# A decoder layer with a mixture of experts: one more expert pass between the last attention segments

## The reference

```
x = LN(x + self_attention(x))            # 16 heads of 16, causal window of 64
x = LN(x + cross_attention(x, ctx))      # relu on q, k, v; causal; + q; LN * gamma + beta
x = LN(x + experts(x))

# experts: tokens in 2 groups of 1024, 8 experts, top 2, capacity 160 per expert and group
pos      = place of each choice in its expert's queue, counted over the whole group
h        = relu(expert_in @ wi[e])       # 160 x 256 @ 256 x 1024
y        = h @ wo[e]                     # 160 x 1024 @ 1024 x 256
```

## Time and profile before

| | |
|---|---|
| median of three executions | 691.75 us (690.23 to 692.27) |
| the profiled execution's own time | 692.64 us |
| its span, first to last instruction | 690.6 us |
| mean granted TensorE clock | 0.909 of full speed |
| PE busy | 543.8 us, 79% |
| PEld busy | 421.6 us, 61% |
| DVE busy | 339.0 us, 49% |
| ACT busy | 218.3 us, 32% |
| POOL busy | 147.5 us, 21% |

### The profile page before, as it was taken

One profiled execution on the slowest core, in us unless ns is written; L12 is line 12 of the kernel. 1 busy time (PEld: TensorE's weight loads), 2 busy tenths in 40 slices (PEclk: granted clock), 3 DMA queues, 4 the chain that ended last, 5 costly groups with the idle time before them and its releaser, 6 DMA issues.

```text
span 690.6 us, 12843 instructions
## 1 busy us (share of the span) xinstructions
PE 543.8 (79%) x5092; PEld 421.6 (61%) x5092; DVE 339.0 (49%) x952; ACT 218.3 (32%) x491; POOL 147.5 (21%) x160
## 2 busy tenths in 40 slices
PE   5074939889898997997988668998687988998970
PEld 4052726656675765665666445777576866787860
DVE  3363615657577676776787547733333101232113
ACT  2000414354254453445445233453110100213103
POOL 4010003011021021031141650001111662322320
PEclk9577879999999999999999887999978989999995
DMA  4999654753935934935384462445555212688214
GB/s 109 202 181 131 211 85 65 96 59 63 121 45 84 113 44 74 113 47 79 48 108 72 84 160 60 152 170 178 203 180 181 62 36 58 191 251 282 32 13 131
DMA packets 56760, 78.97 MB, mean 114 GB/s; under 512 B 9294, under 2 KB 49357, under 8 KB 53628
## 3 DMA queue, kind: packets, MB, share of 16 engines
q1 hardware_dynamic: 42524, 39.64, 35.4%
q10 hardware_dynamic: 8032, 33.21, 15.3%
q0 software_dynamic: 6144, 5.29, 4.7%
HBM read 40.32 MB, written 13.74 MB: 78 GB/s over the span
## 4 chain that ended last, share of the span: by engine, by line
PE 33%; issue 8%; DVE 8%; DMA 3%; ACT 2%; SPq 1%; POOL 1%; ACTq 0%; another core or an unknown queue 0%; POOLq 0%; DVEq 0%
PE work L634 10%; PE work L648 8%; PE work L651 2%; PE work L442 2%; PE pv L560 2%; PE byk L496 1%; DVE negm L913 1%; PE work L436 1%; PE byk L492 1%; PE work L619 1%; DMA arena<-in_ffn_wi 1%; PE nat L496 1%; DVE r_c L984 1%; DVE stats_c L928 1%; PE work L599 1%
## 5 line engine op out<-in xcount | busy, mean ns | idle before, releaser
L913 DVE TENSOR_REDUCE negm<-nat 128x4 f32<-128x512 f32 (+2 forms) x192 | 120.5, 641 | 121.8 <-PE nat L496 116.6
L730 ACT ACTIVATE probs<-byk 128x512 f32<-128x512 f32 (+1 forms) x192 | 106.4, 563 | 131.1 <-PE byk L496 129.1
L496 PE MATMUL nat<-arena 96*128 96x128 bf16 (+2 forms) x512 | 74.9, 250 | 0.0
L496 PE MATMUL byk<-arena 99*128 99x128 bf16 (+2 forms) x512 | 73.1, 245 | 0.0
L1167 POOL TENSOR_TENSOR resk<-fk,parts_k 128x512 f32<-128x512 f32 x8 | 9.3, 1160 | 240.9 <-ACT fk L672 201.2
L492 PE MATMUL nat<-window_q,identb 128*128 128x384 bf16 (+1 forms) x96 | 36.5, 380 | 29.2 <-DMA arena<-parts_k 22.8
L496 PEld LDWEIGHTS nat<-arena 96*128 96x128 bf16 x512 | 47.6, 103 | 17.3 <-issue 3.9
L496 PEld LDWEIGHTS byk<-arena 99*128 99x128 bf16 x512 | 46.3, 100 | 18.6 <-issue 2.3
L492 PE MATMUL byk<-window_k,identb 128*128 128x384 bf16 (+1 forms) x96 | 34.5, 359 | 19.9 <-DMA arena<-mT 19.4
L634 PE MATMUL work<-woT,arena 128*128 128x160 f32 x256 | 46.5, 341 | 4.2 <-issue 4.0
L634 PE MATMUL work<-yn_T,arena 128*128 128x160 f32 x256 | 40.6, 313 | 10.6 <-DMA arena<-in_ffn_wi 6.0
(11 more groups left out here) (189 smaller groups left out, 951.5 us busy)
## 6 DMA issues: line engine op xcount, KB each, us to landing
arena<-parts_q SPq DMA_DIRECT2D x96, 128.0 KB, 5.0
arena<-parts_k SPq DMA_DIRECT2D x96, 128.0 KB, 5.3
arena<-in_ffn_wi ACTq DMA_DIRECT2D x12, 1024.0 KB, 4.9
arena<-in_ffn_wo ACTq DMA_DIRECT2D x12, 1024.0 KB, 8.2
expert_x<-fq ACTq DMA_DIRECT2D x1, 2600.0 KB, 12.6
v_s<-expert_x SPq DMA_DIRECT2D x20, 130.0 KB
xres<-in_x ACTq DMA_DIRECT2D x1, 2048.0 KB, 28.2
token_y<-xres SPq DMA_DIRECT2D x8, 256.0 KB, 2.2
```

The source lines that it names most:

```text
L496: last = nc.tensor.matmul(bank[:, i * w:(i + 1) * w], lhsT, rhs, start=False, stop=(i == heads - 1), skip_group_check=True)
L730: nc.scalar.activation(dst, src, ACT.Exp, scale=0.25).then_inc(exp_ready, 1)
L913: V.tensor_reduce(dst, src, AX, ALU.max, negate=True).then_inc(nat_free[job % 2], 1)
```

## The change

Passes now start at slots 187, 195, 204, 211 and then every 5.4. Pass 0 begins 8 slots earlier, pass 2 is complete in the table when unit 15's last scores are made (at 211), and pass 3 starts right there. Before, pass 2 was the one that stood across that point. The rows of passes 0 and 1 are fetched from slot 179 and 180 instead of 184.5 and 185.5.

Expert 3's weights go to slot 0, once pass 0 has ended, and no longer to slot 3. Expert 4 takes slot 3, once unit 15 has made its last scores; experts 5, 6 and 7 follow on passes 1, 2 and 3 in slots 1, 2 and 0. For the second group expert 7 is still in slot 0, 6 in 2, 5 in 1 and 4 in 3, and experts 3, 2, 1, 0 are loaded after passes 8 to 11. The list `WEIGHTS` holds (expert, slot, pass or none, pair) for each load in this order.

```diff
--- before.py
+++ after.py
@@ -55,6 +55,10 @@
 X_TURN = (1, 1, 1, 1, 2, 2, 2, 3)
 X_BEFORE = {4: 0, 5: 1, 6: 2, 7: 4}
 LOADS = ((-20, 0), (-17.3, 1), (-16, 2), (-5, 3), (-4, 4), (2, 5), (6, 6), (14, 7), (22, 8), (26, 9))
+
+
+WEIGHTS = [(0, 0, None, 0), (1, 1, None, 1), (2, 2, None, 2), (3, 0, 0, 0), (4, 3, None, 3), (5, 1, 1, 1), (6, 2, 2, 2), (7, 0, 3, 0),
+           (3, 0, 8, 0), (2, 2, 9, 2), (1, 1, 10, 1), (0, 3, 11, 3)]
 
 
 PASSES = [(e, 0) for e in range(E)] + [(e, 1) for e in reversed(range(E))]
@@ -106,7 +110,7 @@
             add(end + at, name, n)
         for i in range(TOPK * GT):
             add(end + 3.1 + 0.75 * i, "GS", n, i)
-    begin = [195, 203, 210]
+    begin = [187, 195, 204, 211]
     while len(begin) < len(PASSES) + 1:
         begin.append(begin[-1] + 5.4)
     for x, t in enumerate(begin):
@@ -114,15 +118,13 @@
             add(t, "H0", x)
             add(t + 2, "H1", x)
             add(t + 3.2, "H2", x)
-            add(184.5 + x if x < 2 else begin[x - 2] + 1.9, "EL", x)
+            add(179 + x if x < 2 else begin[x - 2] + 1.9, "EL", x)
             add(begin[0] - 1 if x == 0 else begin[x - 1] + 4, "XT", x)
         if x > 0:
             add(t + 0.8, "EY", x - 1)
             add(t + 1.5, "ES", x - 1)
-    for i in range(WSLOTS):
-        add(first_slot(12 + i) + 30.5, "WL", i)
-        add(begin[i + 1] + 1, "WL", i + WSLOTS)
-        add(begin[E + i + 1] + 1, "WL", E + i)
+    for i, (_, _, prior, pair) in enumerate(WEIGHTS):
+        add(first_slot(12 + pair) + 30.5 if prior is None else begin[prior + 1] + 1, "WL", i)
     for c in range(GB):
         add(begin[E] + 4.2 + 0.1 * c, "FL", 0, c)
         for at, name in ((2.6, "FM"), (2.8, "FR"), (4.5, "FF"), (4.6, "FN"), (4.9, "FS")):
@@ -136,20 +138,16 @@
 PLAN = in_order()
 
 
+def weights_of(x):
+
+    e, n = PASSES[x]
+    i = max(i for i, load in enumerate(WEIGHTS) if load[0] == e and (n == 1 or i < E))
+    return WEIGHTS[i][1], sum(load[1] == WEIGHTS[i][1] for load in WEIGHTS[:i + 1])
+
+
 WORK_SEGS = ("QS", "KS", "VS", "KC", "XC", "QC", "VC", "FQ", "XR", "RT", "MT", "YA", "YB", "Y2", "WO", "GP", "XT", "H0", "H1", "H2", "EY")
 WB = 3
 WORK_TURN = {seg[0:2]: (i % WB, i // WB) for i, seg in enumerate(seg for seg in PLAN if seg[0] in WORK_SEGS)}
-
-
-def weights_of(i):
-
-    e = i if i < E else 2 * WSLOTS + 3 - i
-    return e, e % WSLOTS
-
-
-def weight_turn(e, n):
-
-    return 1 if e < WSLOTS and n == 0 else 2 if e >= WSLOTS else 3
 
 
 def attention_and_experts(nc: bass.Bass, a, out):
@@ -623,33 +621,33 @@
...
                     if name == "H0":
-                        pe.wait_ge(wi_in[e % WSLOTS], 16 * weight_turn(e, n))
+                        pe.wait_ge(wi_in[place], 16 * turn)
                         emptied(pe, "XT", x)
...
@@ -786,13 +784,13 @@
                     nc.scalar.dma_start(wr[:, :, :], a["w_router"]).then_inc(wr_in, 16)
 
             def WL(i, n, layer, b):
-                if i < WSLOTS:
-                    last_t(act, 12 + i)
+                e, place, prior, pair = WEIGHTS[i]
+                if prior is None:
+                    last_t(act, 12 + pair)
                 else:
-                    computed(act, "EY", i - WSLOTS if i < E else i)
-                e, slot_of = weights_of(i)
-                nc.scalar.dma_start(wi[slot_of], a["ffn_wi"][e]).then_inc(wi_in[slot_of], 16)
-                nc.scalar.dma_start(wo[slot_of], a["ffn_wo"][e]).then_inc(wo_in[slot_of], 16)
+                    computed(act, "EY", prior)
+                nc.scalar.dma_start(wi[place], a["ffn_wi"][e]).then_inc(wi_in[place], 16)
+                nc.scalar.dma_start(wo[place], a["ffn_wo"][e]).then_inc(wo_in[place], 16)
 
             def clear(k, n, layer, b):
                 if b == 0:
```

More of the change, by code:

```diff
@@ L625, in handle @@
                 def handle(x, _, layer, b):
-                    e, n = PASSES[x]
+                    place, turn = weights_of(x)
                     if name == "H0":
-                        pe.wait_ge(wi_in[e % WSLOTS], 16 * weight_turn(e, n))
+                        pe.wait_ge(wi_in[place], 16 * turn)
                         emptied(pe, "XT", x)
@@ L640, in EY @@
             def EY(x, _, layer, b):
-                e, n = PASSES[x]
-                pe.wait_ge(wo_in[e % WSLOTS], 16 * weight_turn(e, n))
+                place, turn = weights_of(x)
+                pe.wait_ge(wo_in[place], 16 * turn)
                 for name in ("H0", "H1", "H2"):
@@ L647, in emit @@
                     for f in range(FC):
-                        nc.tensor.matmul(bank[:, 0:D], hT[x % 2][:, f, 0:P], wo[e % WSLOTS][:, f, :], start=(f == 0), stop=(f == FC - 1))
+                        nc.tensor.matmul(bank[:, 0:D], hT[x % 2][:, f, 0:P], wo[place][:, f, :], start=(f == 0), stop=(f == FC - 1))
                     for f in range(FC):
@@ L651, in emit @@
                             mm = nc.tensor.matmul(bank[32 * j:32 * j + REST, D:D + ZW], hT[x % 2][:, f, P:CAP],
-                                                  wo[e % WSLOTS][:, f, j * ZW:(j + 1) * ZW], start=(f == 0), stop=(f == FC - 1),
+                                                  wo[place][:, f, j * ZW:(j + 1) * ZW], start=(f == 0), stop=(f == FC - 1),
                                                   skip_group_check=True)
```

2 lines of the change are left out of this document (1 added, 1 removed).

## The result

The changed kernel took 695.86 us (median of nine runs, 691.85 to 700.2); the kernel before took 690.14 us beside it (median of nine, 686.19 to 699.24). The ratio is 1.009, with a 95% interval of 1.0059 to 1.0121: slower, by about 6 us. The time lies in the range that was given, but the forecast itself, no change at 692.4 us, was wrong. The profiled execution of the changed kernel took 697.16 us, its span is 694.2 us and its mean granted clock 0.895 (before: 692.64, 690.6 and 0.909).

What follows compares the result with a forecast made beforehand. The chain of rows from unit 15 sets pass 8's start, then PE alone bounds the tail. Links of +0.9, +0.6 and -1.8 us plus +1.0 for clock give +0.7: 691.75 to 692.4 us, range 688.8 to 696.5.

Steps and rivals of the forecast that it cites:

- first rival: Before unit 15's last scores: expert 3's load delays the maxima rows; +4.3 us, 696 us; 28% including any other longer link.
- a wait of `byk` for the maxima rows: Sign that the forecast is wrong: before unit 15's last scores, PE waits for that unit's maxima rows.
- last scores near 489.1 us: Sign that the forecast is right: unit 15's last scores come within 1.5 us of 489.1; after 492 means wrong.
- the chain of rows: Unit 15's norms, router, choices, row sends, landing and fetch set pass 8's transposes, which move by -0.3 us.
- third rival: Whole kernel faster by a pass, if PE's list set the end: about 682 us; chance 2%.
- Link 1: Up to unit 15's last scores: 3.63 us more PE work, partly offset by waits that go; +0.9 us.
- the margin of 4 us: Before unit 15's last scores: about 4 us from the maxima copy's issue until PE wants it, so no delay counted.
- a term of 0: Maxima copy beside expert 3's load, in different queues: it waits for packets, not 2 MB; 6.3 us by the worst row.
- Link 2: Unit 15's last scores to first row send: the 6 us gap on a weight load remains; +0.6 us, bounds -2 and +4.
- Link 3: First row send to pass 8's transposes: five sends instead of six behind the second output; -1.8 us, from -3.5 to 0.
- The clock at pass 8: Pass 8 starts at 1.2 GHz after a PE wait of 15 us; +1.0 us.
- The rest of the tail: After pass 8 PE alone runs one pass after another, 10.55 us each; nothing changes.

Runs made afterwards that it cites:

- e6_late_load: The changed kernel with expert 3's load issued later, after unit 15's maxima rows; 695.27 us, ratio 1.005 to the kernel before.
- e11_again: The changed kernel, unaltered, measured a third time, on the fourth chip; 698.56 us, ratio 1.0072 to the kernel before.
- e12_weights_only_again: The kernel before with only the new weight slots, passes at their old starts, repeated on the fourth chip; 683.65 us, ratio 0.985.
- e3_load_first: The changed kernel with expert 4's load issued right after unit 15's last scores, ahead of expert 6's; 676.31 us, ratio 0.9878 to the kernel before.
- e1_again: The changed kernel, unaltered, measured again on the second chip; 686.31 us, ratio 1.0016 to the kernel before.
- e4_passes_only: The kernel before with the new pass starts and old weight slots, expert 3's load directly behind unit 15's last scores; 685.87 us, ratio 1.001.
- e5_warm: The changed kernel with 60 matmuls of unused result ahead of PE's wait for pass 8's rows; 697.54 us, ratio 1.0102 to the kernel before.
- e7_rows_first: The changed kernel with all 16 row sends of the second group ahead of the outputs of passes 5 and 6; 693.04 us, ratio 1.001.
- e8_best: The kernel before with the new weight slots, old pass starts, and all second-group row sends ahead of the outputs; 690.4 us, ratio 0.9986.
- after: The changed kernel in its first measurement and trace, against the kernel before; 695.86 us, ratio 1.009.
- e9_before_again: The kernel before, unaltered, one run on the third chip for a second trace; 686.63 us.
- e2_weights_only: The kernel before with only the new weight slots, passes at their old starts, on the second chip; 677.12 us, ratio 0.9829.

## Why the prediction was right or wrong

That the time lies in the range is partly luck. The range was drawn wide for the first rival, and the kernel before came out 1.6 us lower beside the changed one than in its first three executions; 1.009 times the 691.75 us that the forecast started from would be 698.0, above 696.5. The forecast of no change was wrong, and the sign of it that the prediction had named, a wait of `byk` for the maxima rows, is in every trace of the changed kernel. The other sign, last scores near 489.1 us, was met (489.7) only because the stretch ahead of `YA 12` was 3.3 us shorter.

The mechanism it was built on was right: the chain of rows through unit 15's norms, router and dispatch sets the end, and not the number of passes on PE. The pass taken out of PE's list came back as a wait of 18.6 us at `XT 8` (forecast about 15), and the third rival, faster by a pass, is excluded by that row. Its steps:

- **Link 1, the load of expert 3: failed.** The prediction counted nothing for the collision and kept it as the first rival, with a wait of 2 us and 1.6 us for the clock. Measured: a wait of 1.62 us, and 3.3 us in all by `e6_late_load` against `e11_again`. With the late load the link is 78.0 us, 0.8 more than in before and 1.3 more than in `e12_weights_only_again` on the same chip, and the sum of the other terms had been +0.9. So these terms stood about as said (waits for norms gone, 1.1 us for expert 2 where 0.9 was said), and the missing 3 us are the collision, near the 3.6 us at which the rival had priced it. The step behind the error was the margin of 4 us from the issue of the copies to PE's need. By the trace it was 6.0 us (458.29 to 464.26, where the wait begins), longer than thought, and even so too short: PE was released 7.6 us after the first issue, where the median copy lands in 1.9 us. The Trainium skill (DMA: Bandwidth & Descriptors, Queues, rings and completion order) says that DMA engines take turns between queues, packet by packet, and from this the prediction had drawn a term of 0. The trace doesn't bear out that conclusion: the copies waited although they were in another queue. What the turns cost each packet no trace here shows. The trace of before had a warning that was not read: its longest landings, 8.7 to 10.3 us, are those of the three copies from 57.7 us on, behind a load of 256 KB in their own queue and beside one of 256 KB in ACT's, and PE waited 7.6 us for them. (A slip without effect: if every wait goes and none is new, the terms give -0.6 and not -0.9.)
- **Link 2, last scores to the first `GS`: right.** The gap of 6.0 us moved from pass 3 to pass 4 with its half clock (3.57 us for the first group, 6.0 us for the wait, as in before), unit 15's norm wait fell from 2.3 to 0.75 us (0.5 said), and the link came out at +0.41 where +0.6 was said. `e3_load_first` took the gap away and gained 1.4 points of ratio on the same chip.
- **Link 3, first `GS` to `XT 8`: failed.** -1.8 us was said and +0.73 measured; in the other traces with the gap in front of pass 4 and the outputs where they were it is 38.6 us at the least (`e1_again`) and 40.8 at the most (`e6_late_load`), before 39.3 and 39.1. The step that failed is that pass 5's output would end 4.5 us after the first `GS`. It ended after 7.4, and POOL started on it after 8.7. Two things are in it. `H0` of pass 6 and most of the output behind it ran at half clock after the wait at `GP` (3.54 us at 536.97, clock 0.50; before it was the row below), which makes it 13.2 us from `GP` to the output instead of 12.0. And the first `GS` came 4.5 us after `GP` instead of 5.9. The hold-ups of 3.8 us that passes 5 and 6 had in before did shrink to 0.3 us at pass 6, but POOL waited 3.86 and 1.28 us for outputs all the same, and the `GS` that was saved went there. The second of these waits is not PE's doing: its output ended at 556.7, and DVE began on it at 560.02, for a release that the profile calls remote; in `e1_again` there is no such wait, and the link is 1.5 us shorter. In the trace of before, for comparison:

```profile
531.15 0.26 PE L609 MATMUL work<-choice,tri 128*128 128x128 bf16 x1 [3.64 <-issue]
...
535.20 1.87 PE L634 MATMUL work<-yn_T,arena 128*128 128x160 f32 x12 [0.57 <-issue]
```

  What the link does without the half clock is seen in `e3_load_first` and `e4_passes_only`, where pass 6 stands the same way against `GP` but starts at full clock behind the same wait of 2.2 us. POOL starts on the first output 6.0 us after the first `GS` (518.72 and 531.31), the second needs no wait, and the link is 36.4 and 36.2 us, below the 37.5 that the prediction said; `e1_again` on the same chip, with half clock at pass 6, has 38.6. The rows of `e3_load_first`:

```profile
516.94 1.87 PE L632 MATMUL work<-woT,arena 128*128 128x160 f32 x12 [0.57 <-issue]
```

```profile
524.73 1.56 POOL L1217 DMA_INDIRECT token_y<-ynat_s,target  x1 [1.13 <-DVE ynat_s L1076]
```

  So the term that was missing in this link is the clock at pass 6. Why it fell there in one kernel and not in the other, after equal waits, no run tested.

- **The clock at pass 8: right in kind, somewhat small.** +1.0 was said and +1.58 measured in the first pair; over the six traces that have both the gap behind the last scores and a wait of 4 us or more at `XT 8` (three of the changed kernel, `e4_passes_only`, `e5_warm`, `e6_late_load`) it is 12.71 to 13.87 us, against 12.29 and 10.61 for before. The step took the price from one wait of 6 us; behind 18.6 us the half clock lasted longer, over `XT`, `H0` and on to 585 us.
- **The rest of the tail** was unchanged, as said: 65.65 us from `XT 9` to `XT 15` in both.

Together: 3.0 us too little in link 1, 2.5 in link 3, 0.6 at the clock and 0.2 in the tail, less 0.2 too much in link 2, is the 6.2 us by which the sum of the table, 6.87, is above the 0.7 that was said. The largest gain of the matter was missed altogether: the prediction saw that expert 3's new place had not removed the gap, but did not ask what it does without the new starts of passes.

## What to carry to other kernels

When work is moved ahead of a point, ask of each wait behind that point whether it is gone or has merely passed to the next user. Here the late weights of expert 3 became the late weights of expert 4, since PE arrived there one pass further on and ACT's queue was in the same order. And when a large load starts at another point, be it only because the pass that it waits for has moved, list the small transfers that now start beside it and have a reader close behind. In the seven traces here with a load beside them the reader of the three 8 KB copies was released 7.4 to 8.6 us after the first was issued; the 2 us of the median landing is no margin there.

## What the runs showed of the hardware

- **PE was held up while POOL sent rows.** In `e7_rows_first` 64 small matmuls that take 1.1 us otherwise were spread over some 8.3 us, with stops of up to 1.1 us that wait for no semaphore; in `e8_best` 5.3 us went in eight such stops. In before two passes lost 3.8 us in the same way, in after 0.3 us. The four traces of the second chip have no such stop in this stretch, although POOL sends the same rows there. So the rows alone don't make it; the cause was not tested and stays open.
- **Granted clock.** A wait of 1.6 us was followed by a stretch at 0.57 in two traces of the changed kernel and by full clock in the third (`e1_again`), a wait of 4.2 us after 13 us of matmuls by one at 0.58, and a wait of 18.6 us by a longer one at 0.50; in `e9_before_again`, without a wait, the same pass ran at full clock (1.87 us for its first group).
- **One program, several times.** From `YA 12` to `YA 13` the changed kernel took 33.0 us in two traces and 26.9 in another, and its ratio to the kernel before was 1.009, 1.0016 and 1.0072 in three measurements. All four traces of the second chip, of four different kernels, have a wait of 3.0 to 3.1 us for a load of `parts_q` in this stage, where the others wait 2.5 us or more for ACT and 1.3 for DVE's sums (`e1_again`, `e2_weights_only` against `after`, `e12_weights_only_again`). On that chip the changed kernel is only 1.6 us above the weights' half in link 1 (75.1 and 73.6), on the fourth 4.6 us (81.3 and 76.7), which fits the smaller loss. Why the chip decides it I don't know; the effect is as large as the one that was asked for.
- **A pass of the tail** takes 11.13 us and not 10.55 in four of the six intervals from `XT 9` to `XT 15`, before and after alike, as the gap behind the transposes is 1.15 us there instead of 0.57. The prediction's 10.55 was read from one that had the short gap; the cancelling on both sides made it harmless.
